# Output projection of a cross-attention block: seven block products per batch in place of eight

## The chip, the cores and the metric

The kernel runs on one core of a Trainium2 chip. The metric is the device time of one execution in microseconds (us), lower is better. Engines: PE is TensorE (matmuls), DVE is VectorE, ACT is ScalarE, POOL is GpSimd; the SP queue issues all DMA transfers here.

## The reference, cut to what matters

```
q = lora_linear(x, Wq, Aq, Bq)      # x: (8, 256, 1024), Wq: (1024, 1024)
k, v = lora_linear(traces, ...)     # 8 key/value heads of 32
attn = softmax(q k^T / sqrt(32)); context = attn v      # 32 query heads
out = lora_linear(context, Wo, Ao, Bo)                  # (8, 256, 1024)
return x + out
```

`lora_linear(x, W, A, B)` is `x @ W + 2 (x @ A @ B)` with rank 16. Everything is float32. The kernel folds the low-rank part into the weights first (W + 2AB), so that the last step is one product of the context, 256 x 1024 per batch, with a 1024 x 1024 matrix, called Wo below.

## The kernel before, in words

Every operand of a matmul is split into a high part (rounded to the format of the matmul) and a low part (the rest), and a product is the sum of three: high by high, high by low, low by high. So each 128-row step of a contraction is three matmuls.

The kernel has three stages. A prologue folds the weights and projects the first inputs. Then comes an attention stage of eight batches, cut into slots (32 per batch); in the last batch's slots the fold of Wo runs too, and the output projection of batch 0. At the end stands the output projection of batches 1 to 7 by itself.

Names that the change touches:

- `w_hl` (high, low) holds in its columns 512 to 1023 the right half of Wo, and `wkv_hl` the left half (`wo_piece`, line 282). The columns 0 to 511 of `w_hl` are free by then and take the context of two batches, `ctx_raw`, loaded by `load_ctx` (line 349). POOL makes Wo's low parts (line 644).
- `first_split` (line 696): POOL splits batch 1's context into `x_hl` (called `o_parts[1]`) in slots 28 and 31 to 33 of the last batch; its last step counts `o_ready`, on which PE's batch 1 waits.
- `place_max` (line 709), `normalize` (line 971, multiplies the context of one key/value head, "unit", by the row sums and counts `ctx_done`), `copy_turned` (line 964), `first_rows` (line 1013, adds x to the rows of batch 0). DVE's `slot` (line 1022) runs them in fixed slots: `first_rows` in slots 29, 33 and 37, `copy_turned` in 30 and 34, `normalize` of units 5, 6 and 7 in slots 31, 35 and 39.
- PE's `context` (line 1181) of unit 7 stands in slot 36, behind all of batch 0's output products, and waits until `normalize` of unit 6 has freed its bank.
- `out_batch` of PE (line 1296): four groups of 24 matmuls (`out_step`, line 1196), each 128 rows by 512 columns with the contraction over 1024: the two halves of the rows by the two halves of the columns. Each group has its own bank of PSUM, and two batches use different banks.
- `o_high` (ACT, line 864) and `o_low` (DVE, line 1069): one instruction each of 128 x 2048 elements splits the next batch's context into `c_hl` or `x_hl`. `rows_out` (DVE, line 1075): four additions of a bank and x's rows per batch. SP's `out_batch` (line 610) loads the next context but one, stores the rows and loads the next rows.

The order on each engine is written out by hand: an engine takes its instructions in program order, and a wait holds up all that stands behind it on that engine.

## Time and profile before

| | us |
|---|---|
| median of 3 runs (lowest, highest) | 716.83 (715.74, 717.96) |
| the profiled execution | 718.58 |
| its span, first to last instruction | 716.8 |
| PE busy | 697.4 |
| ACT busy | 446.3 |
| DVE busy | 400.9 |
| POOL busy | 310.3 |

The span is that of the profiled execution alone; 1.8 us lie around it. PE's busy time is modelled from starts of pipelined matmuls, so 97% says that it always has work queued, not that it runs at its peak.

### The profile page before, as it was taken

Reading aid. Unit: us, or ns where it says so; the run is one execution under the profiler, and the core shown is the slowest. Engines: PE = TensorE matmul, PEld = TensorE weight load, DVE = VectorE, ACT = ScalarE, POOL = GpSimd, SP = SyncE. Lnnn points to the kernel's source line nnn. Section 1 sums busy time; section 2 is a strip of 40 time slices with the busy share of each in tenths; the row PEclk is TensorE's granted clock in tenths of the full one; section 3 lists DMA queues with packets and bytes.
Section 4 is the critical chain, followed back from the end, with each engine's and each line's share of the span. In section 5 each row is a group of like instructions: output and inputs, shape, how many; then the busy total and the mean of one; then the engine's idle time right before and its main releaser. Section 6 shows DMA issues by size and latency. Waiting matters only on the chain.

```text
span 716.8 us, 16086 instructions
## 1 busy us (share of the span) xinstructions
PE 697.4 (97%) x5122; PEld 596.6 (83%) x5122; DVE 400.9 (56%) x805; ACT 446.3 (62%) x1418; POOL 310.3 (43%) x282
## 2 busy tenths in 40 slices
PE   6989999999999999999999999999899999999998
PEld 6768888888888888888888888887667788888886
DVE  4946877676566667567566656766674222122211
ACT  2546888888788788788888888888885111001100
POOL 3663832853573375277248338536878100000000
PEclk9999999999999999999999999999999999999999
DMA  6777675776577477666756757767675553354231
GB/s 231 274 222 210 196 199 148 192 192 180 153 187 202 136 198 199 168 159 186 197 140 187 196 146 191 196 175 193 179 221 198 170 176 110 125 176 160 74 117 59
DMA packets 103747, 125.77 MB, mean 175 GB/s; under 512 B 9248, under 2 KB 85280, under 8 KB 103712
## 3 DMA queue, kind: packets, MB, share of 16 engines
q1 hardware_dynamic: 103712, 125.34, 61.0%
q8 instruction: 17, 0.28, 0.2%
q14 instruction: 18, 0.15, 0.1%
HBM read 87.29 MB, written 38.01 MB: 175 GB/s over the span
## 4 chain that ended last, share of the span: by engine, by line
PE 87%; DMA 7%; DVE 2%; SPq 2%; POOL 1%; issue 1%; ACT 0%; DVEq 0%
PE banks L1131 35%; PE banks L1200 24%; PE banks L1149 10%; PE banks L1189 8%; PE banks L1176 8%; DMA r_rows<-turned_sb 3%; PE banks L1167 2%; PE banks L1116 1%; DMA probs_t<-b4kv 1%; DMA stage<-b4q 1%; POOL k_stack L654 1%; SPq L346 1%; DMA probs_t<-wq 1%; PE banks L1118 1%; DMA scales<-r_rows 1%
## 5 line engine op out<-in xcount | busy, mean ns | idle before, releaser
L943 DVE TENSOR_REDUCE neg_max<-banks 128x2 f32<-128x512 f32 x256 | 176.4, 690 | 130.3 <-PE banks L1149 128.8
L793 ACT ACTIVATE banks<-banks,neg_max 128x256 f32<-128x256 f32 x512 | 231.1, 455 | 15.5 <-DVE neg_max L943 15.5
L714 POOL TENSOR_TENSOR q_stack<-turned_sb,head_mask 8x512 fp32r<-8x512 f32 x128 | 135.6, 1060 | 202.1 <-DVE turned_sb L969 196.7
L804 ACT ACTIVATE probs_t<-banks 128x512 f32<-128x512 f32 x256 | 154.6, 604 | 74.0 <-PE banks L1176 72.4
L1131 PE MATMUL banks<-x_hi,w_hi 128*128 128x256 f32 x512 | 144.5, 282 | 0.9 <-POOL w_lo L644 0.9
L1131 PE MATMUL banks<-x_lo,w_hi 128*128 128x256 f32 x512 | 144.5, 282 | 0.0
L1131 PE MATMUL banks<-x_hi,w_lo 128*128 128x256 f32 x512 | 144.3, 282 | 0.0
L1149 PE MATMUL banks<-k_stack,q_stack 96*128 96x256 f32 x512 | 109.9, 296 | 3.9 <-DMA q_stack<-q_parts 2.5
L793 ACT ACTIVATION_READ_ACCUMULATOR banks<-banks,neg_max 128x1 f32 x512 | 108.6, 212 | 0.0
L1176 PE MATMUL banks<-q_stack,k_stack 104*128 104x512 f32 x256 | 107.7, 421 | 0.0
L1149 PEld LDWEIGHTS banks<-k_stack,q_stack 96*128 96x128 f32 x512 | 79.2, 190 | 31.6 <-ACT banks L793 19.8
L1131 PEld LDWEIGHTS banks<-x_lo,w_hi 128*128 128x128 f32 x512 | 97.4, 190 | 7.3
L1131 PEld LDWEIGHTS banks<-x_hi,w_hi 128*128 128x128 f32 x512 | 97.3, 190 | 1.4 <-issue 1.0
L1131 PEld LDWEIGHTS banks<-x_hi,w_lo 128*128 128x128 f32 x512 | 96.9, 189 | 0.0
L1083 DVE TENSOR_TENSOR raw<-banks,stage 128x512 f32<-128x512 f32 x28 | 19.4, 692 | 112.5 <-PE banks L1200 112.5
L1189 PE MATMUL banks<-probs_t,v_sb 128*32 128x256 f32 x1024 | 68.5, 385 | 0.0
L1176 PEld LDWEIGHTS banks<-q_stack,k_stack 104*128 104x128 f32 x256 | 48.4, 189 | 1.3 <-issue 0.8
L1189 PEld LDWEIGHTS banks<-probs_t,v_sb 128*32 128x32 f32 x1024 | 26.7, 109 | 20.7 <-issue 1.8
L867 ACT ACTIVATE x_hi<-w_hi 128x2048 fp32r<-128x2048 f32 x3 | 5.8, 1917 | 60.8 <-PE banks L1200 60.8
L693 POOL TENSOR_TENSOR c_lo<-raw,c_hi 128x512 fp32r<-128x512 f32 x32 | 41.3, 1291 | 2.5
L936 DVE TENSOR_TENSOR q_stage<-banks,q_stage 128x256 fp32r<-128x256 f32 x64 | 27.1, 424 | 25.7 <-ACT q_stage L777 25.2
L1131 PE MATMUL banks<-wkv_hi,c_hi 128*128 128x256 f32 x128 | 36.3, 284 | 1.1 <-DVE k_stage L931 1.1
(104 smaller groups left out, 1284.5 us busy)
## 6 DMA issues: line engine op xcount, KB each, us to landing
q_stack<-q_parts SPq DMA_DIRECT2D x192, 128.0 KB, 3.7
q_parts<-q_stage SPq DMA_DIRECT2D x64, 256.0 KB, 2.6
raw<-ct SPq DMA_DIRECT2D x32, 256.0 KB, 4.3
raw<-xt SPq DMA_DIRECT2D x32, 256.0 KB, 4.2
scales<-r_rows SPq DMA_DIRECT2D x64, 128.0 KB
context<-ctx_stage SPq DMA_DIRECT2D x64, 128.0 KB, 2.3
stage<-xn SPq DMA_DIRECT2D x16, 512.0 KB, 4.2
w_hi<-context SPq DMA_DIRECT2D x14, 512.0 KB, 6.0
```

The lines of the kernel that those rows point to most:

```text
L693: nc.gpsimd.tensor_tensor(cols[1], raw[:, j, :], cols[0], ALU.subtract).then_inc(ready, 1)
L714: nc.gpsimd.tensor_tensor(q_stack[rows, u % RING, heads], turned_sb[rows, u % 2].unsqueeze(1).broadcast_to([M_ROWS, 2, S]), head_mask[rows ...
L793: last = nc.scalar.activation(score_bank[c % 2][:, S * h:S * (h + 1)], score_bank[c % 2][:, S * h:S * (h + 1)], ACT.Exp, bias=neg_max[:, u ...
L804: nc.scalar.activation(probs_t[:, u % 2, t, 2 * hp:2 * hp + 2, :].rearrange("p a b -> p (a b)"), st_bank[j % 2], ACT.Exp, scale=-1.0).then ...
L936: nc.vector.tensor_tensor(q_stage[:, i % 2, 1, :], src, q_stage[:, i % 2, 0, :], ALU.subtract).then_inc(proj_out, 1)
L943: nc.vector.tensor_reduce(out=neg_max[:, u % 2, 2 * c:2 * c + 2], in_=score_bank[c % 2].rearrange("p (h t) -> p h t", h=2), axis=AXIS, op= ...
L1083: nc.vector.tensor_tensor(out_rows[h][:, cols], out_bank(i, h, half), x_rows[h][:, cols], ALU.add).then_inc(o_out, 1)
L1131: mm = nc.tensor.matmul(proj_bank[bank][:, 0:S], lhs, rhs, start=(k == 0), stop=(k == GROUP_MM - 1))
L1149: last = nc.tensor.matmul(score_bank[c % 2][:, S * h:S * (h + 1)], q_stack[0:3 * HD, u % RING, 2 * hp + h, P * qh:P * (qh + 1)], k_stack[0 ...
L1176: nc.tensor.matmul(st_bank[j % 2], k_stack[0:KM, u % NG, P * t:P * (t + 1)], q_stack[0:KM, u % RING, 2 * hp:2 * hp + 2, :].rearrange("p a ...
L1189: last = nc.tensor.matmul(ctx_bank[HD * h:HD * (h + 1), :], v_sb[:, t, HD * (u % NG):HD * (u % NG + 1)], probs_t[:, u % 2, t, h, :], start ...
L1200: mm = nc.tensor.matmul(bank, o_parts[i][t_part][:, kt, P * qh:P * (qh + 1)], wo_piece(w_part, kt, half), start=(k == 0), stop=(k == GROUP ...
```

## The change

For batches 2 to 7 the product of the context A (as 2 x 2 blocks of 128 x 512) and Wo (as B, 2 x 2 blocks of 512 x 512) is made from seven block products: A11 B11, A12 B21, S4 B22, A22 T4, S1 T1, S2 T2, S3 T3, with S1 = A21 + A22, S2 = S1 - A11, S3 = A11 - A21, S4 = A12 - S2 and T1 = B12 - B11, T2 = B22 - T1, T3 = B22 - B12, T4 = T2 - B21. Each block product is 12 matmuls of 512 columns. Batch 1 stays as it was, but for the order of its groups: both row halves of the right columns first.

POOL forms the S, ACT and DVE split each of the seven left factors (`form_high`, `form_low`) one product after the other, and DVE, POOL and ACT put the seven results together (`take_product`, `add_rows`, `copy_first`). The T are built once: T1's twelve pieces by DVE in slots 30 to 38 of the last attention batch, T2 and T4 by DVE after it, T3 by POOL. Banks, order and buffers are shown in the diff, cut to its core.

```diff
+PRODUCTS = (("A11", "B11", 0), ("S4", "B22", 1), ("S2", "T2", 6), ("A12", "B21", 7), ("S3", "T3", 2),
+            ("S1", "T1", 3), ("A22", "T4", 4))
+P1, P3, P6, P2, P7, P5, P4 = range(7)
+ADDED = ("S1", "S2", "S4", "S3")
+T1_SLOTS = (30, 31, 32, 32, 33, 34, 34, 35, 36, 36, 37, 38)
...
+        form_room = [q_stack[:, i].rearrange("p a b -> p (a b)") for i in range(4)] + [
+            k_stack[:, 4 * i:4 * i + 4].rearrange("p a b -> p (a b)") for i in range(2)] + [
+            q_stage[:].rearrange("p a b c -> p (a b c)")]
+        added_room = dict(zip(ADDED, [t[:].rearrange("p a b -> p (a b)") for t in (v_new, v_sb, ctx_stage, scales)]))
...
+        wo_forms = {"B11": [t[:, 0:4, :] for t in wkv_hl], "B21": [t[:, 4:8, :] for t in wkv_hl],
+                    "B12": [t[:, 0:4, 512:1024] for t in w_hl], "B22": [t[:, 4:8, 512:1024] for t in w_hl],
+                    "T1": [t[:].rearrange("p (a b) n -> p a (b n)", b=2) for t in c_hl],
+                    "T2": [t[:, 0:4, 512:1024] for t in w_hl],
+                    "T3": [w_hl[1][:, 4 * i:4 * i + 4, 0:512] for i in range(2)],
+                    "T4": [t[:].rearrange("p (a b) n -> p a (b n)", b=2) for t in x_hl]}
+        t1_raw = t4_raw = w_sum
+        t3_raw, t2_raw = (probs_t[:, i].rearrange("p a b n -> p (a b n)").rearrange("p (a n) -> p a n", a=4)
+                          for i in range(2))
+        u2, u3 = (t2_raw[:, i, :] for i in range(2))
...
+                for i in range(2):
+                    wait(ctx_stored[i], DMA * (1 + 4 * NG // 2))
+                wait(first_lo, 3)
+                wait(o_ready, 1)
+                load_ctx(3, 1)
...
+            for h in range(2):
+                wait(o_out, 7 + h)
+                sp.dma_start(out[1, P * h:P * (h + 1), :], out_rows[h]).then_inc(out_stored[h], DMA)
+                load_rows(2, h)
...
-                    wait(o_ready, v)
+                    wait(form_lo, products_to(v, P4))
...
+            pool.wait_ge(w_lo_pool, sums_to(FOLDS - 1))
+            pool.wait_ge(ctx_mm, (NB - 1) * NG + 7)
+            nc.gpsimd.tensor_tensor(t3_raw, wo_forms["B22"][0].bitcast(F32), wo_forms["B12"][0].bitcast(F32),
+                                    ALU.subtract).then_inc(t3_step, 1)
+            pool.wait_ge(t3_step, 1)
+            nc.gpsimd.tensor_tensor(t3_raw, t3_raw, wo_forms["B12"][1].bitcast(F32), ALU.subtract).then_inc(t3_step, 1)
+            def add_forms(v):
+                def a(name):
+                    return quarter(ctx_raw[v % 2], name)
+                pool.wait_ge(ctx_in[v % 2], (v + 1) // 2 * 2 * DMA)
+                if v > 2:
+                    pool.wait_ge(form_lo, products_to(v - 1, P5))
+                for n, (name, one, two, op) in enumerate((
+                        ("S1", a("A21"), a("A22"), ALU.add), ("S2", added("S1"), a("A11"), ALU.subtract),
+                        ("S4", a("A12"), added("S2"), ALU.subtract), ("S3", a("A11"), a("A21"), ALU.subtract))):
+                    nc.gpsimd.tensor_tensor(added(name), one, two, op).then_inc(form_added, 1)
+                    pool.wait_ge(form_added, 4 * (v - 2) + n + 1)
+            def add_rows(v):
+                def add(i, l, what):
+                    x = row_quarter(x_rows, i, l)
+                    nc.gpsimd.tensor_tensor(x, x, what, ALU.add).then_inc(rows_added, 1)
+                pool.wait_ge(copied, v - 1)
+                pool.wait_ge(rows_in[0], (v + 1) * DMA)
+                add(1, 1, p1_copy[:])
+                pool.wait_ge(p3_added, v - 1)
+                pool.wait_ge(u_done, 2 * (v - 2) + 1)
+                add(1, 2, u2)
+                pool.wait_ge(u_done, 2 * (v - 2) + 2)
+                pool.wait_ge(rows_in[1], (v + 1) * DMA)
+                add(2, 2, u3)
+                add(2, 1, u3)
+                pool.wait_ge(rows_added, 4 * (v - 1))
+            pool.wait_ge(ctx_done, NB * NG)
+            for i in range(2):
+                pool.wait_ge(ctx_stored[i], DMA * (1 + NB * NG // 2))
+            add_forms(2)
+            pool.wait_ge(t3_step, 2)
+            nc.gpsimd.tensor_tensor(t3_raw, t3_raw, wo_forms["B22"][1].bitcast(F32), ALU.add).then_inc(t3_step, 1)
+            pool.wait_ge(t3_step, 3)
+            pool.wait_ge(t_hi, 3)
+            nc.gpsimd.tensor_tensor(wo_forms["T3"][1], t3_raw, wo_forms["T3"][0], ALU.subtract).then_inc(t3_lo, 1)
+            for v in range(2, NB):
+                if v + 1 < NB:
+                    add_forms(v + 1)
+                add_rows(v)
...
-            def o_high(v):
-                act.wait_ge(ctx_in[v % 2], (v + 1) // 2 * 2 * DMA)
-                act.wait_ge(o_mm, 4 * (v - 1))
-                nc.scalar.activation(o_parts[v % 2][0][:].rearrange("p (a b) n -> p a (b n)", b=2), ctx_raw[v % 2],
-                                     ACT.Copy).then_inc(o_hi_done, 1)
+            def t_high(name, raw_tile, steps, count):
+                act.wait_ge(steps, count)
+                nc.scalar.activation(wo_forms[name][0], raw_tile, ACT.Copy).then_inc(t_hi, 1)
+            def form_high(v, p):
+                if v > 2:
+                    act.wait_ge(product_mm, products_to(v - 1, p))
+                name = PRODUCTS[p][0]
+                if name[0] == "A":
+                    act.wait_ge(ctx_in[v % 2], (v + 1) // 2 * 2 * DMA)
+                else:
+                    act.wait_ge(form_added, 4 * (v - 2) + ADDED.index(name) + 1)
+                nc.scalar.activation(form(p, 0), form_source(v, p), ACT.Copy).then_inc(form_hi, 1)
+            def copy_first(v):
+                act.wait_ge(product_mm, products_to(v, P1))
+                need(act, rows_added, 4 * (v - 3) + 1)
+                need(act, u_done, 2 * (v - 3) + 1)
+                nc.scalar.activation(p1_copy[:], product_bank(P1), ACT.Copy).then_inc(copied, 1)
+            act.wait_ge(st_mm, NB * SLOTS)
+            form_high(2, P1)
+            act.wait_ge(o_mm, 4)
+            t_high("T1", t1_raw[:], t_step, 12)
+            form_high(2, P3)
+            form_high(2, P6)
+            form_high(2, P2)
+            act.wait_ge(o_mm, 6)
+            act.wait_ge(t3_step, 1)
+            t_high("T2", t2_raw, t_step, 14)
+            form_high(2, P7)
+            form_high(2, P5)
+            for i in range(2):
+                act.wait_ge(q_stored[i], NB * 4 * DMA)
+            form_high(2, P4)
+            t_high("T3", t3_raw, t3_step, 3)
+            act.wait_ge(o_mm, 8)
+            t_high("T4", t4_raw[:], t_step, 16)
             for v in range(2, NB):
-                o_high(v)
+                for p in range(7):
+                    if p == P1:
+                        copy_first(v)
+                    if v + 1 < NB:
+                        form_high(v + 1, p)
...
+            def t1_piece(n):
+                op, kt = divmod(n, 4)
+                place = t1_raw[:, kt, :]
+                if n == 0:
+                    dve.wait_ge(w_lo_pool, sums_to(FOLDS - 1))
+                if op == 0:
+                    nc.vector.tensor_tensor(place, wo_forms["B12"][0][:, kt, :].bitcast(F32),
+                                            wo_forms["B11"][0][:, kt, :].bitcast(F32), ALU.subtract).then_inc(t_step, 1)
+                else:
+                    dve.wait_ge(t_step, n - 3)
+                    name, how = (("B12", ALU.add), ("B11", ALU.subtract))[op - 1]
+                    nc.vector.tensor_tensor(place, place, wo_forms[name][1][:, kt, :].bitcast(F32), how).then_inc(t_step, 1)
+            def t_total(base, taken, place, steps):
+                dve.wait_ge(t_step, steps)
+                nc.vector.tensor_tensor(place, wo_forms[base][0].bitcast(F32), taken, ALU.subtract).then_inc(t_step, 1)
+                dve.wait_ge(t_step, steps + 1)
+                nc.vector.tensor_tensor(place, place, wo_forms[base][1].bitcast(F32), ALU.add).then_inc(t_step, 1)
+            def t_low(name, raw_tile, highs):
+                dve.wait_ge(t_hi, highs)
+                nc.vector.tensor_tensor(wo_forms[name][1], raw_tile, wo_forms[name][0], ALU.subtract).then_inc(t_lo_dve, 1)
+            def form_low(v, p):
+                dve.wait_ge(form_hi, products_to(v, p))
+                nc.vector.tensor_tensor(form(p, 1), form_source(v, p), form(p, 0), ALU.subtract).then_inc(form_lo, 1)
...
+                if last:
+                    for n in range(len(T1_SLOTS)):
+                        if T1_SLOTS[n] == s:
+                            t1_piece(n)
...
+            def put_out(v, p, i, l, added):
+                if (i, l) in ((1, 1), (2, 2)):
+                    dve.wait_ge(out_stored[i - 1], (v + 1) * DMA)
+                dve.wait_ge(rows_added, 4 * (v - 2) + added)
+                nc.vector.tensor_tensor(row_quarter(out_rows, i, l), product_bank(p),
+                                        row_quarter(x_rows, i, l), ALU.add).then_inc(o_out, 1)
+            def take_product(v, p):
+                dve.wait_ge(product_mm, products_to(v, p))
+                if p == P3:
+                    x = row_quarter(x_rows, 1, 2)
+                    dve.wait_ge(rows_in[0], (v + 1) * DMA)
+                    nc.vector.tensor_tensor(x, product_bank(P3), x, ALU.add).then_inc(p3_added, 1)
+                if p == P6:
+                    dve.wait_ge(copied, v - 1)
+                    need(dve, rows_added, 4 * (v - 3) + 2)
+                    nc.vector.tensor_tensor(u2, product_bank(P6), p1_copy[:], ALU.add).then_inc(u_done, 1)
+                if p == P2:
+                    put_out(v, P2, 1, 1, 1)
+                if p == P7:
+                    dve.wait_ge(u_done, 2 * (v - 2) + 1)
+                    need(dve, rows_added, 4 * (v - 2))
+                    nc.vector.tensor_tensor(u3, product_bank(P7), u2, ALU.add).then_inc(u_done, 1)
+                if p == P5:
+                    put_out(v, P5, 2, 2, 3)
+                    put_out(v, P5, 1, 2, 2)
+                if p == P4:
+                    put_out(v, P4, 2, 1, 4)
+            dve.wait_ge(ctx_mm, NB * NG)
+            t_total("B22", t1_raw[:], t2_raw, 12)
+            t_low("T1", t1_raw[:], 1)
+            dve.wait_ge(t_lo_dve, 1)
+            t_total("B21", t2_raw, t4_raw[:], 14)
+            form_low(2, P1)
+            plain_rows(0)
+            plain_rows(1)
+            dve.wait_ge(t3_step, 2)
+            t_low("T2", t2_raw, 2)
+            form_low(2, P3)
+            form_low(2, P6)
+            plain_rows(2)
+            form_low(2, P2)
+            form_low(2, P7)
+            form_low(2, P5)
+            plain_rows(3)
+            t_low("T4", t4_raw[:], 4)
+            form_low(2, P4)
+            for v in range(2, NB):
+                for p in range(7):
+                    take_product(v, p)
+                    if v + 1 < NB:
+                        form_low(v + 1, p)
...
-            out_batch(1, 1, True)
-            pe.wait_ge(o_out, 4)
-            with pe.Fori(1, NB // 2) as pair:
-                for i in range(2):
-                    out_batch(pair * 2 + i, i, False)
+            pe.wait_ge(o_ready, 1)
+            for n in range(4):
+                if n == 2:
+                    pe.wait_ge(ctx_done, NB * NG)
+                for k in range(GROUP_MM):
+                    out_step(1, out_bank(n), n % 2, 1 - n // 2, k)
+            def product(v, p):
+                weight = PRODUCTS[p][1]
+                pe.wait_ge(form_lo, products_to(v, p))
+                if v == 2 and p == P6:
+                    pe.wait_ge(t_lo_dve, 2)
+                if v == 2 and p == P7:
+                    pe.wait_ge(t3_lo, 1)
+                if v == 2 and p == P4:
+                    pe.wait_ge(t_lo_dve, 3)
+                if v == 2 and p in (P1, P7):
+                    pe.wait_ge(o_out, 4 if p == P1 else 8)
+                if v > 2:
+                    free = {P1: (copied, v - 2), P3: (p3_added, v - 2), P6: (u_done, 2 * (v - 3) + 1),
+                            P2: (o_out, 4 * (v - 1) + 1), P7: (u_done, 2 * (v - 2)),
+                            P5: (o_out, 4 * (v - 1) + 3), P4: (o_out, 4 * v)}[p]
+                    pe.wait_ge(*free)
+                for k in range(12):
+                    kt, part = divmod(k, 3)
+                    w_part, a_part = ((0, 0), (0, 1), (1, 0))[part]
+                    mm = nc.tensor.matmul(product_bank(p), form_room[p][:, 512 * a_part + P * kt:512 * a_part + P * (kt + 1)],
+                                          wo_forms[weight][w_part][:, kt, :],
+                                          start=(k == 0), stop=(k == 11))
+                mm.then_inc(product_mm, 1)
+            for v in range(2, NB):
+                for p in range(7):
+                    product(v, p)
```

## Rows read from the trace of the kernel before

**Rows 1.** The page's busy times, and its chain that ended last, by engine.

```profile
PE 697.4 (97%) x5122; PEld 596.6 (83%) x5122; DVE 400.9 (56%) x805; ACT 446.3 (62%) x1418; POOL 310.3 (43%) x282
...
PE 87%; DMA 7%; DVE 2%; SPq 2%; POOL 1%; issue 1%; ACT 0%; DVEq 0%
```

**Rows 2.** The chain from 560 us to the end: start, us, what.

```profile
559.95 1.00 PE banks L1189 x16
560.95 152.60 PE banks L1200 x672
713.55 0.02 issue
713.58 0.69 DVE raw L1083
```

**Rows 3.** The windows view: us, PE, PEld, DVE, ACT, POOL busy, granted clock, DMA share, GB/s.

```profile
10.00:15.00 5.00, 1.35 (x4) 1.20 (x5) 4.51 (x3) 1.26 (x2) 3.32 (x2) 0.83 0.70 267
15.00:17.00 2.00, 2.00 (x9) 1.74 (x8) 0.41 (x1) 0.84 (x2) 0.00 (x0) 0.58 0.00 0
...
590.00:600.00 10.00, 10.00 (x46) 8.29 (x45) 1.25 (x2) 0.00 (x0) 0.00 (x0) 1.00 0.39 130
```

**Rows 4.** Groups by line: engine, operation, out<-in, shape, count, busy, mean ns, idle before.

```profile
L644 POOL TENSOR_TENSOR w_lo<-w_sum,w_hi 128x512 fp32r<-128x512 f32 x16 | 20.6, 1285 | 10.2 <-ACT w_hi L770 9.7
L1083 DVE TENSOR_TENSOR raw<-banks,stage 128x512 f32<-128x512 f32 x28 | 19.4, 692 | 112.5 <-PE banks L1200 112.5
...
L770 ACT ACTIVATE w_hi<-w_sum 128x512 fp32r<-128x512 f32 x16 | 10.2, 636 | 3.5 <-DVE w_sum L913 3.5
...
L1073 DVE TENSOR_TENSOR c_lo<-w_hi,c_hi 128x2048 fp32r<-128x2048 f32 x3 | 6.9, 2292 | 3.2 <-ACT c_hi L867 3.2
...
L867 ACT ACTIVATE x_hi<-w_hi 128x2048 fp32r<-128x2048 f32 x3 | 5.8, 1917 | 60.8 <-PE banks L1200 60.8
```

**Rows 5.** POOL's timeline at four moments at which it meets DVE.

```profile
18.08 1.53 POOL L644 TENSOR_TENSOR wkv_lo<-w_sum,wkv_hi 128x512 fp32r<-128x512 f32 x1 [4.69 <-ACT wkv_hi L770]
...
24.79 5.84 POOL L654 TENSOR_TENSOR q_stack<-stage,q_stack 32x1024 fp32r<-32x1024 f32 x2 [0.63 <-DVE q_stack L881]
...
154.80 2.54 POOL L714 TENSOR_TENSOR q_stack<-turned_sb,head_mask 8x512 fp32r<-8x512 f32 x2 [2.28 <-DVE turned_sb L969]
...
532.76 4.03 POOL L644 TENSOR_TENSOR w_lo<-w_sum,w_hi 128x512 fp32r<-128x512 f32 x3
```

**Rows 6.** DVE's timeline at the same four moments.

```profile
17.79 0.68 DVE L981 TENSOR_TENSOR c_lo<-raw,c_hi 128x512 fp32r<-128x512 f32 x1
18.39 0.68 DVE L913 SCALAR_TENSOR_TENSOR w_sum<-banks,probs_t 128x512 f32<-128x512 f32 x1
...
25.08 3.30 DVE L885 TENSOR_TENSOR q_stack<-stage,q_stack 64x1024 fp32r<-64x1024 f32 x1
...
156.58 1.30 DVE L981 TENSOR_TENSOR x_lo<-raw,x_hi 128x512 fp32r<-128x512 f32 x1
...
535.58 0.69 DVE L913 SCALAR_TENSOR_TENSOR w_sum<-banks,raw 128x512 f32<-128x512 f32 x1
```

**Rows 7.** POOL's timeline, 546 to 559 us.

```profile
546.78 1.04 POOL L701 TENSOR_TENSOR x_hi<-w_hi,ones 128x512 fp32r<-128x512 f32 x1
547.91 1.29 POOL L704 TENSOR_TENSOR x_lo<-w_hi,x_hi 128x512 fp32r<-128x512 f32 x1
549.27 2.16 POOL L714 TENSOR_TENSOR q_stack<-turned_sb,head_mask 8x512 fp32r<-8x512 f32 x2
...
557.35 1.29 POOL L704 TENSOR_TENSOR x_lo<-w_hi,x_hi 128x512 fp32r<-128x512 f32 x1
```

**Rows 8.** DVE's timeline, 542 to 562 us: start, us, engine, line, what.

```profile
547.41 0.42 DVE L969 COPY turned_sb<-banks 104x256 f32<-104x256 f32 x1 [1.46 <-PE banks L1167]
...
550.79 0.42 DVE L975 TENSOR_TENSOR ctx_stage<-banks,scales 128x256 f32<-128x256 f32 x1 [2.85 <-DMA scales<-r_rows]
552.37 0.69 DVE L1019 TENSOR_TENSOR stage<-banks,stage 128x512 f32<-128x512 f32 x1 [1.15 <-PE banks L1200]
...
555.66 0.41 DVE L975 TENSOR_TENSOR ctx_stage<-banks,scales 128x256 f32<-128x256 f32 x1
560.06 0.69 DVE L1019 TENSOR_TENSOR stage<-banks,stage 128x512 f32<-128x512 f32 x1 [3.98 <-PE banks L1200]
561.08 0.42 DVE L975 TENSOR_TENSOR ctx_stage<-banks,scales 128x256 f32<-128x256 f32 x1 [0.33 <-PE banks L1189]
```

**Rows 9.** DMA issues: what, queue, count, KB each, median us to landing.

```profile
context<-ctx_stage SPq DMA_DIRECT2D x64, 128.0 KB, 2.3
```

**Rows 10.** PE's timeline, 10 to 30 us: its first work behind its longest idle time there.

```profile
13.65 1.19 PE L1116 MATMUL banks<-probs_t,half_ident 128*128 128x256 f32 x2 [4.26 <-POOL k_stack L654]
```

More of the change, by code:

```diff
@@ L211, in xattn @@
         ctx_done = sem("ctx_done")
-        o_hi_done = sem("o_hi_done")
+        form_added = sem("form_added")
+        form_hi = sem("form_hi")
+        form_lo = sem("form_lo")
+        t_step = sem("t_step")
+        t3_step = sem("t3_step")
+        t_hi = sem("t_hi")
+        t_lo_dve = sem("t_lo_dve")
+        t3_lo = sem("t3_lo")
+        product_mm = sem("product_mm")
+        copied = sem("copied")
+        rows_added = sem("rows_added")
+        p3_added = sem("p3_added")
+        u_done = sem("u_done")
         first_hi = sem("first_hi")
@@ L301, in lora_of, with out_bank, product_bank, products_to @@
             return lora_q if f < FOLD_O else lora_o
-        def out_bank(i, qh, half):
-            return banks[:, ((0, 6, 1, 7), (2, 3, 4, 5))[i][2 * qh + half], :]
+        def out_bank(n):
+            return banks[:, 2 + n, :]
+        def product_bank(p):
+            return banks[:, PRODUCTS[p][2], :]
+        def products_to(v, p):
+            return 7 * (v - 2) + p + 1
+        def quarter(raw_tile, name):
+            i, j = int(name[1]) - 1, int(name[2]) - 1
+            return raw_tile.rearrange("p a (h n) -> p a h n", h=2)[:, 2 * j:2 * j + 2, :, P * i:P * (i + 1)]
+        def form_source(v, p):
+            name = PRODUCTS[p][0]
+            if name[0] == "A":
+                return quarter(ctx_raw[v % 2], name)
+            return added(name)
+        def added(name):
+            return added_room[name].rearrange("p (a h n) -> p a h n", a=2, h=2)
+        def form(p, part):
+            return form_room[p][:, 512 * part:512 * (part + 1)].rearrange("p (a h n) -> p a h n", a=2, h=2)
+        def row_quarter(rows, i, l):
+            return rows[i - 1][:, 512 * (l - 1):512 * l]
         def need(engine, semaphore, value):
@@ L1067, in _ @@
                 dve.sem_inc(out_stored[h], DMA)
-            def o_low(v):
-                i = v % 2
-                dve.wait_ge(o_hi_done, v - 1)
-                hi, lo = (t[:].rearrange("p (a b) n -> p a (b n)", b=2) for t in o_parts[i])
-                nc.vector.tensor_tensor(lo, ctx_raw[i], hi, ALU.subtract).then_inc(o_ready, 1)
-            def rows_out(v, i):
-                for h in range(2):
-                    dve.wait_ge(rows_in[h], v * DMA + DMA)
-                    dve.wait_ge(out_stored[h], v * DMA + DMA)
-                    for half in range(2):
-                        dve.wait_ge(o_mm, v * 4 + (2 * h + half + 1))
-                        cols = slice(512 * half, 512 * (half + 1))
-                        nc.vector.tensor_tensor(out_rows[h][:, cols], out_bank(i, h, half),
-                                                x_rows[h][:, cols], ALU.add).then_inc(o_out, 1)
@@ L1086, in _, with plain_rows @@
-            dve.wait_ge(o_ready, 1)
-            for v in range(1, NB):
-                if v + 1 < NB:
-                    o_low(v + 1)
-                rows_out(v, v % 2)
+            def plain_rows(n):
+                half, h = 1 - n // 2, n % 2
+                if half == 1:
+                    dve.wait_ge(rows_in[h], 2 * DMA)
+                    dve.wait_ge(out_stored[h], 2 * DMA)
+                dve.wait_ge(o_mm, 4 + n + 1)
+                cols = slice(512 * half, 512 * (half + 1))
+                nc.vector.tensor_tensor(out_rows[h][:, cols], out_bank(n), x_rows[h][:, cols],
+                                        ALU.add).then_inc(o_out, 1)
@@ L1294, in _ @@
                 slot(NB - 1, s, False, True)
-            def out_batch(v, i, first):
-                pe.wait_ge(o_ready, v)
-                for qh in range(2):
-                    if first and qh:
-                        pe.wait_ge(ctx_done, NB * NG)
-                    for half in range(2):
-                        if not first:
-                            pe.wait_ge(o_out, v * 4 + (2 * qh + half - 7))
-                        for k in range(GROUP_MM):
-                            out_step(i, out_bank(i, qh, half), qh, half, k)
```

23 lines of the change are left out of this document (12 added, 11 removed).

## The prediction

> **What bounds the kernel now.** I read the page's busy times first, then the chain that ended last, then the chain in order of time for the end. PE is busy for 97% of the span and carries 87% of the chain [rows 1]. From 560.95 us on the chain is one piece, 672 matmuls of the output projection in 152.60 us, with 0.02 us of idle, one DVE addition and a store of some 2.5 us behind it [rows 2]. So here PE's matmuls alone set the time, at 152.60 / 672 = 0.227 us each, and the other engines have room: in ten of these microseconds DVE works 1.25 and POOL not at all [rows 3]. The chain passes through `context` of unit 7 at 559.95 [rows 2]. All that the change adds comes before or after that point, on DVE, POOL and ACT.
>
> **What it removes.** Batches 2 to 7 take 7 x 12 = 84 matmuls in place of 96, so 6 x 12 = 72 fall away: 72 x 0.227 = 16.3 us, all on PE's path. That is certain if PE is never kept waiting.
>
> **What it adds when all runs smoothly.** A block product is 12 x 0.227 = 2.72 us and a batch 19.0. Per batch ACT gets eight operations of 512 columns (0.64 each, 5.1 us), DVE seven low parts and seven additions (0.69 each at most [rows 4], 9.7 us), POOL eight additions (1.28 each, 10.3 us). A left factor is split a whole batch ahead, right behind the product that freed its room, so about 13 us of slack hide it. From batch 3 on I cost this at nothing; its cover is that slack. Context loads now hang on the last low part of a batch, some 19 us before they are needed, with a store and a row load beside them as before: nothing. The last addition and the half-row store at the end stay: nothing. The longer unrolled code I bound between 0 and 1 us and take 0, as batch 1, unrolled already, sits inside the same 152.60 us.
>
> **Where it costs: DVE and POOL in each other's way.** Rows 5 and 6 have to be read together. DVE's `L885` at 25.08 starts inside two POOL operations and takes 3.30 us; its work of 1024 columns is about 1.1. It ends 2.2 us late, when the first POOL operation is through. The POOL pair takes 5.84, and 1.1 of that is DVE's, for which the second stood still: 2.4 us for each. `L981` at 156.58 takes 1.30 in place of 0.68 and ends 0.54 behind POOL's pair, whose end is 157.34. The other way round, POOL's `L644` at 18.08 takes 1.53 in place of 1.28, for `L981` at 17.79 was still at work. But `L913` at 535.58 takes 0.69 in the middle of POOL's 4.03 us of work: it reads a bank and one tensor of SBUF [rows 5, 6]. So a DVE operation on two SBUF tensors and a POOL operation exclude each other, each for its whole length, and whoever waits gets the next turn; additions from PSUM are exempt. Page "SBUF — State Buffer" of the Trainium skill, section "SBUF: two separate sides", calls the pair of ports an exclusive lock, "held for the full instruction"; by that rule the trace agrees for lengths up to 2.4 us, and no row shows a longer one.
>
> All of T1 to T4, every low part of a factor, every S and every row sum on POOL now lies in this queue. Prices of a turn: DVE 0.60 for 512 columns (starts of successive operations at 17.79 and 18.39 [rows 6]) and 2.2 for 2048 (2.29 less the overlap [rows 4]); POOL 1.24 for 512 (1.28 [rows 4] less overlap). POOL on 2048 is not in the trace. Lower bound 4 x 1.04 = 4.2 from the scaling operation, upper bound 4 x 1.29 = 5.2 [rows 7]; I take 4.9, 1.28 plus three more times the 1.2 that lie between 512 and the 2.4 us of 1024 columns. Page "GPSIMD Engine Reference" of the Trainium skill, section "Elementwise — side-by-side cycle accounting", has 4.5 us for this operation; by it the end would come about 1.6 us earlier than by the rows.
>
> I write the queue out, with 0.1 us where an engine waits for its own last result, and with turns alternating where both want one.
>
> 1. **To `context` of unit 7.** DVE's first T1 piece is at 547.8, behind `copy_turned` [rows 8]. Behind `normalize` of unit 5 (at 550.8 [rows 8]) stand pieces 1 to 6 and then `normalize` of unit 6, and each piece waits for one POOL operation of `place_max` and `first_split`, eight operations that follow each other almost without a gap from 549.27 to 558.64 [rows 7]: piece 1 ends at 552.6, piece 3 at 556.1, piece 6 at 561.2, `normalize` at 561.6 in place of 556.1 [rows 8]. PE wants it at 559.95 [rows 2]: it waits 1.7, and batch 1 starts at 562.7. POOL's last low part of batch 1, `o_ready`, comes at 562.5, just in time.
> 2. **To `ctx_done`.** Piece 7 ends at 563.1. POOL's two first T3 steps, 4.9 each, alternate with pieces 8 and 9: 574.1. `first_rows` (0.6), pieces 10 and 11 (1.2) and `normalize` of unit 7 (0.4) end at 576.3. PE's third group of batch 1 waits for it: due at 562.7 + 48 x 0.227 = 573.6, so 2.8 lost. Queued behind are SP's last context store (0.3 + 2.3 us [rows 9]) and with it POOL's S of batch 2, from 579.
> 3. **To the first product.** Four passes of T2 and T4 and T1's low part are 5 x 2.2, four S of POOL stand between them (4 x 1.24), then P1's low part: 11.0 + 5.0 + 0.6 = 16.6, done at 593.0. PE is through with batch 1 at 587.2: 5.8 lost. It works on P1 until 595.7.
> 4. **To the second product.** T3's third step 592.9 to 597.8, T2's low part to 600.0, T3's low part (its high part, 1.92 on ACT [rows 4], is ready at 599.9) to 604.9, P3's low part to 605.5. PE starts P3 at 605.6, 9.9 us late by the rows at full clock.
> 5. **After it.** The six low parts left of batch 2 come at 0.6 each with 2.72 us of need each: no stall. T4's low part and POOL's S of batch 3 make DVE some 6 us late, less than the slack of a factor. Per later batch the queue holds 8 x 1.3 + 7 x 0.6 = 14.6 of 19.0 us, so it catches up.
> 6. **The clock.** PE idles 4.26 us before 13.65 [rows 10], and the granted clock is 0.83 in 10 to 15 us and 0.58 in 15 to 17: partly at 1.2 in place of 2.4 GHz, which loses 0.17 x 5 + 0.42 x 2 = 1.7 us of full-speed work [rows 3]. The waits of 5.8 and 9.9 us are longer than that idle time. Bounds: nothing, or 1.7 us for each. For the one ahead of P3 I take 1.7, as its row is so near; the one ahead of P1 costs nothing, because P3 waits for DVE anyway.
>
> Sum: -16.3 + 1.7 + 2.8 + 5.8 + 9.9 + 1.7 = +5.6; counted from P3's start (41 products in 111.5 us, the clock, 3.2 us of tail) the span ends at 722.1, or +5.3. The profiled execution took 718.58 with its span of 716.8; with the change it would take 724. It stands 1.75 above the median of the runs, 716.83, so the median becomes 722. Should P3's low part get its turn ahead of T3's, a matter of 0.2 us, PE starts P3 at 600.7, waits 2.8 for P6, and the end is near 718.5. I forecast **721.0**.
>
> **Rivals.**
> - *DVE keeps its turn* as long as its operations follow each other without a wait. No row shows both queues full. Then pieces 2 and 3, 5 to 7 and so on go together, `normalize` comes in time, but POOL's last low part of batch 1 comes at 567.7 only, PE starts batch 1 6.8 late and P3 at 600.1 us: 716.9, no change, give or take 2. Chance 0.27.
> - *The turns are not whole ones*: long POOL operations let DVE in between, or the three engines' work falls more luckily than I wrote. With no collision at all DVE has P1's low part at about 574 and P3's at about 580, ahead of PE's 582.7 and 585.4, and the full saving stands: 716.8 - 16.3, a median of 700.5. Against it stand all of [rows 5, 6]; for it, that none shows an operation of 4.9 us. Chance 0.18, over 700 to 713.
> - *The queue never recovers*: POOL lags into batch 4 and later, and stalls come back in each batch. It decides from the point where the queue holds over 19.0 us a batch, and I count 14.6. Then over 724: chance 0.05.
> - My forecast, alternating turns: 0.5, from 718.5 to 723.5.
>
> **How the numbers follow.** A measurement of this kernel tells 0.3%, 2.15 us, from no change. Slower by more (over 719.0): most of the forecast and the last rival, 0.5. Within it (714.7 to 719.0): most of the first rival and the lucky end of mine, 0.28. Faster: the rest, 0.22. The range runs from 713.0, below which only the second rival lies, to 724.0. It takes in POOL's bounds (4.2 gives about 2.8 us less, 5.2 about 1.2 more) and the clock's.
>
> **What the profile after would show.** If I am right: T1's pieces of over 1 us while POOL works, two of them near 5; `context` of unit 7 waiting for `normalize`; PE's P3 of batch 2 waiting for DVE some 5 to 10 us; `t_low` and `t_total` well over 2.3 us, POOL's long steps up to 7; from P6 of batch 2 on, gapless PE, 2.72 us a product; a granted clock below 1 behind the longest wait. Wrong: T1's pieces at 0.68 beside a busy POOL, or PE without a gap at batch 2, and then 700.5.

## The result, and the profile after

The changed kernel takes 720.31 us (median of 17 runs, 718.42 to 723.64), the kernel before, measured beside it, 717.96 (17 runs). The ratio is 1.0039, 95% interval 1.0026 to 1.0052: slower by 2.35 us, within the range and 0.7 us below the number forecast. The 72 matmuls are gone and their 16.3 us with them; 18.7 us came back.

The profiled execution took 719.19 us with a span of 717.4, 0.6 more than the span of before. Busy time and the chain by engine, from the page of the changed kernel:

```profile
PE 685.9 (96%) x5050; PEld 585.6 (82%) x5050; DVE 484.6 (68%) x878; ACT 470.7 (66%) x1464; POOL 414.5 (58%) x334
...
PE 78%; DMA 7%; DVE 7%; issue 2%; POOL 2%; SPq 2%; ACT 1%; DVEq 0%; POOLq 0%
```

Against [rows 1], PE is busy for 11.5 us less, but its share of the chain fell from 87% to 78%, and DVE's rose from 2% to 7%. DVE's busy time grew by 83.7 us for 73 more instructions, 1.15 us each, and POOL's by 104.2 for 52, 2.0 each. DVE's 73 are, on balance, 72 of 512 columns and one of 2048, which alone take some 0.7 us each on average; POOL's are 48 of 512 and four of 2048, some 1.5 us each on average (estimates from 0.68 and 2.29, and from 1.28 and the 4.62 of the last experiment). So both engines are busy for longer than their new work is: a first sign that some of it is waiting.

The chain in order of time shows where it left PE. P1, P3, P6, P2, P7, P5 and P4 below are the seven block products in the order in which PE makes them: A11 B11, S4 B22, S2 T2, A12 B21, S3 T3, S1 T1 and A22 T4. These are rows of the chain of the changed kernel from 565 us on (start, us, what):

```profile
565.06 5.08 DVE w_sum L1200
570.15 0.60 DVE stage L1185
...
572.31 1.71 DMA context<-ctx_stage
...
574.24 1.41 POOL v_new L848
...
587.58 4.98 DVE q_stack L1216
592.55 1.20 DVE raw L1277 x2
593.75 2.20 DVE w_lo L1212
595.95 4.95 DVE q_stack L1216
...
600.95 113.20 PE banks L1567 x492
...
714.17 0.69 DVE raw L1285
```

Where [rows 2] had one piece of 672 matmuls, there is now one of 492 (41 products) from 600.95 on. Ahead of it the chain runs through DVE, and two of its steps are low parts of 512 columns, work of 0.6 us, that last 5. PE's own timeline, 556 to 625 us, has just four rows with idle time ahead of them (in brackets, with what released PE):

```profile
558.82 1.07 PE L1433 MATMUL banks<-probs_t,v_sb 128*32 128x256 f32 x16 [0.17 <-DVE ctx_stage L1141]
...
572.34 0.50 PE L1444 MATMUL banks<-wkv_hi,x_hi 128*128 128x512 f32 x1 [1.34 <-DVE ctx_stage L1141]
...
592.61 1.22 PE L1567 MATMUL banks<-wkv_hi,q_stack 128*128 128x512 f32 x2 [9.08 <-DVE q_stack L1216]
...
600.95 1.22 PE L1567 MATMUL banks<-w_hi,q_stack 128*128 128x512 f32 x2 [3.27 <-DVE q_stack L1216]
```

They are the four waits of the prediction: `context` of unit 7, the third group of batch 1, P1 and P3. Together 13.9 us. None follows, to the end.

The reason is in two timelines, to be read side by side. DVE's, changed kernel, 556 to 602 us (start, us, engine, line, operation, out<-in, shape, count):

```profile
560.04 10.11 DVE L1200 TENSOR_TENSOR w_sum<-w_sum,wkv_lo 128x512 f32<-128x512 f32 x2
...
572.21 2.27 DVE L1206 TENSOR_TENSOR probs_t<-w_hi,w_sum 128x2048 f32<-128x2048 f32 x1
574.52 3.27 DVE L1208 TENSOR_TENSOR probs_t<-probs_t,w_lo 128x2048 f32<-128x2048 f32 x1
...
584.41 3.24 DVE L1208 TENSOR_TENSOR w_sum<-w_sum,wkv_lo 128x2048 f32<-128x2048 f32 x1
587.58 4.98 DVE L1216 TENSOR_TENSOR q_stack<-w_hi,q_stack 128x512 fp32r<-128x512 f32 x1
...
593.68 2.27 DVE L1212 TENSOR_TENSOR w_lo<-probs_t,w_hi 128x2048 fp32r<-128x2048 f32 x1
595.88 5.02 DVE L1216 TENSOR_TENSOR q_stack<-ctx_stage,q_stack 128x512 fp32r<-128x512 f32 x1
600.82 0.68 DVE L1216 TENSOR_TENSOR q_stack<-v_sb,q_stack 128x512 fp32r<-128x512 f32 x1
```

POOL's, the same stretch:

```profile
556.40 1.49 POOL L775 TENSOR_TENSOR x_hi<-w_hi,ones 128x512 fp32r<-128x512 f32 x1
557.96 1.61 POOL L778 TENSOR_TENSOR x_lo<-w_hi,x_hi 128x512 fp32r<-128x512 f32 x1
559.52 5.07 POOL L832 TENSOR_TENSOR probs_t<-w_hi 128x2048 f32<-128x2048 f32 x1
564.67 4.93 POOL L835 TENSOR_TENSOR probs_t<-probs_t,w_lo 128x2048 f32<-128x2048 f32 x1
574.24 1.40 POOL L848 TENSOR_TENSOR v_new<-w_hi 128x512 f32<-128x512 f32 x1 [4.64 <-DMA context<-ctx_stage]
575.71 3.22 POOL L848 TENSOR_TENSOR v_sb<-v_new,w_hi 128x512 f32<-128x512 f32 x1
...
582.31 3.19 POOL L848 TENSOR_TENSOR scales<-w_hi 128x512 f32<-128x512 f32 x1
585.58 6.42 POOL L875 TENSOR_TENSOR probs_t<-probs_t,w_lo 128x2048 f32<-128x2048 f32 x1
594.09 6.26 POOL L878 TENSOR_TENSOR w_lo<-probs_t,w_lo 128x2048 fp32r<-128x2048 f32 x1 [2.09 <-ACT w_lo L995]
```

Two pieces of T1 take 10.11 us beside POOL's first two steps of T3, and the two low parts of 5 us lie under its last two. A pass of 2048 columns takes 2.27 alone (572.21) and 3.24 to 3.37 when an S of POOL must go first; the S takes 3.2 in place of 1.3. The time shows as busy time of the operation that stands still, not as a wait: DVE's "busy" 4.98 us hold 0.6 of work.

### The profile page after: what moved, and what is told of

Its sections match the earlier page's. It is cut to its first block, busy times and chain, and to the rows that moved or that the text cites. A ratio compares the mean times of both kernels' runs of the same rounds, so it can differ in the third digit from the quotient of the medians.

```text
span 717.4 us, 16217 instructions
## 1 busy us (share of the span) xinstructions
PE 685.9 (96%) x5050; PEld 585.6 (82%) x5050; DVE 484.6 (68%) x878; ACT 470.7 (66%) x1464; POOL 414.5 (58%) x334
## 4 chain that ended last, share of the span: by engine, by line
PE 78%; DMA 7%; DVE 7%; issue 2%; POOL 2%; SPq 2%; ACT 1%; DVEq 0%; POOLq 0%
PE banks L1375 35%; PE banks L1567 16%; PE banks L1393 9%; PE banks L1433 8%; PE banks L1420 7%; DMA r_rows<-turned_sb 3%; PE banks L1411 2%; DVE w_sum L1200 1%; DVE q_stack L1216 1%; DMA q_parts<-q_stage 1%; DMA q_stack<-q_parts 1%; PE banks L1360 1%; DMA probs_t<-b4kv 1%; POOL k_stack L728 1%; PE banks L1362 1%
## 5 line engine op out<-in xcount | busy, mean ns | idle before, releaser
L856 POOL TENSOR_TENSOR stage<-stage,probs_t 128x512 f32<-128x512 f32 x18 | 27.2, 1527 | 29.6 <-DVE probs_t L1304 19.8
L1567 PE MATMUL banks<-wkv_hi,q_stack 128*128 128x512 f32 x96 | 31.3, 408 | 9.1 <-DVE q_stack L1216 9.1
L757 POOL TENSOR_TENSOR x_hi<-raw,ones 128x512 fp32r<-128x512 f32 x28 | 31.5, 1126 | 11.6 <-PE banks L1375 8.3
```

Of the source, the lines that this page charges most:

```text
L757: nc.gpsimd.tensor_tensor(hi, raw[:, j, :], ones[:, 0:1].broadcast_to([P, 2 * S]), ALU.mult).then_inc(hi_done, 1)
L856: nc.gpsimd.tensor_tensor(x, x, what, ALU.add).then_inc(rows_added, 1)
L1567: mm = nc.tensor.matmul(product_bank(p), form_room[p][:, 512 * a_part + P * kt:512 * a_part + P * (kt + 1)], wo_forms[weight][w_part][:, k ...
```

## The experiments

**T3 on 16 of every 512 columns.** It leaves out nearly all of T3, so what P7 multiplies with is not T3; all instructions and waits remain. If POOL's long operations are the cause, this alone brings back the saving. The rival: DVE's own list before P1 (five passes of 2048) is too long whatever POOL does.

```diff
-            nc.gpsimd.tensor_tensor(t3_raw, wo_forms["B22"][0].bitcast(F32), wo_forms["B12"][0].bitcast(F32),
+            few = slice(0, 16)
+            nc.gpsimd.tensor_tensor(t3_raw[:, :, few], wo_forms["B22"][0][:, :, few].bitcast(F32), wo_forms["B12"][0][:, :, few].bitcast(F32),
                                     ALU.subtract).then_inc(t3_step, 1)
...
```

> POOL's four T3 operations work on 16 of every 512 columns; most of T3 is left out, all waits and all else stay. Queue theory (an addition of two SBUF tensors on DVE and a POOL operation exclude each other): the four holds of 4.4 us go, norm of unit 7 comes 8 us sooner, PE has no gap at batch 2 (0 to 1 us in place of 9.1 and 3.3), the span falls from 717.4 to about 700. Rival, DVE's own list of work is too long (11 us of T2, T4 and T1 passes ahead of the first low part): T3 is not on DVE, so the gaps ahead of P1 and P3 stay above 8 us in sum and the span above 711.

Measured: 700.95 us (4 runs, 700.67 to 703.15), ratio to the kernel before 0.9785 [0.9753, 0.9816], span 698.9. DVE's timeline:

```profile
559.54 1.54 DVE L1201 TENSOR_TENSOR w_sum<-w_sum,wkv_lo 128x512 f32<-128x512 f32 x2
...
575.35 3.27 DVE L1209 TENSOR_TENSOR w_sum<-w_sum,wkv_lo 128x2048 f32<-128x2048 f32 x1
578.55 0.81 DVE L1217 TENSOR_TENSOR q_stack<-w_hi,q_stack 128x512 fp32r<-128x512 f32 x1
```

The pieces take 1.54 in place of 10.11 and P1's low part 0.81 in place of 4.98. The passes beside an S keep their 3.27 and do no harm: PE runs from 559.40 through batch 1 and 42 products without a gap. The rival fell. Four operations of POOL, some 18 us of its time, cost the whole saving and more: 2.35 slower than the kernel before with them, 17.1 faster without them.

**Fills in place of T3.** Is it that POOL is busy, or that it reads SBUF? Each step of T3 becomes two fills with zero of its 2048 columns, 3.7 us in all, that write as before but read nothing. T3 is left out.

```diff
-            nc.gpsimd.tensor_tensor(t3_raw, wo_forms["B22"][0].bitcast(F32), wo_forms["B12"][0].bitcast(F32),
-                                    ALU.subtract).then_inc(t3_step, 1)
-            pool.wait_ge(t3_step, 1)
-            nc.gpsimd.tensor_tensor(t3_raw, t3_raw, wo_forms["B12"][1].bitcast(F32), ALU.subtract).then_inc(t3_step, 1)
+            marks = [0, 0]
+            for _ in range(2):
+                nc.gpsimd.memset(t3_raw, 0.0).then_inc(t3_step, 1)
+                marks[0] += 1
+                pool.wait_ge(t3_step, marks[0])
...
```

> Each of POOL's four T3 operations is replaced by two fills of the same 2048 columns with zero, about 3.7 us in all: POOL is busy for nearly as long, but reads nothing. T3 is left out (zeros). If the two engines exclude each other over reading: DVE's T1 pieces beside the fills take 0.68 us, PE has no gap at batch 2 and the span is near 700, as with the thinned T3. If any POOL operation shuts DVE out: two T1 pieces take about 2 us each (a fill apiece), and 5 to 8 us of gaps stay, span 707 to 713.

Measured: 700.79 us (4 runs, 700.52 to 704.77), ratio 0.9791 [0.9751, 0.983], span 698.7. POOL's timeline:

```profile
558.88 3.68 POOL L834 MEMSET probs_t<- 128x2048 f32 x2
562.62 3.70 POOL L838 MEMSET probs_t<- 128x2048 f32 x2
```

DVE's, beside it:

```profile
559.40 1.28 DVE L1209 TENSOR_TENSOR w_sum<-w_sum,wkv_lo 128x512 f32<-128x512 f32 x2
...
562.74 2.27 DVE L1215 TENSOR_TENSOR probs_t<-w_hi,w_sum 128x2048 f32<-128x2048 f32 x1
```

Under 7.4 us of fills, DVE's additions of two SBUF tensors take 0.64 and 2.27, their time alone. So POOL does not shut DVE out by being busy or by writing; what the fills lack is the reading of SBUF. The fills run in pairs of 1.85 us; had each shut DVE out, the two pieces would have taken about 2 us each.

**T3 in four operations a step.** The same work in turns a quarter as long. If turns go by whole instructions, P1 and P3 come much earlier.

```diff
-            nc.gpsimd.tensor_tensor(t3_raw, wo_forms["B22"][0].bitcast(F32), wo_forms["B12"][0].bitcast(F32),
-                                    ALU.subtract).then_inc(t3_step, 1)
-            pool.wait_ge(t3_step, 1)
-            nc.gpsimd.tensor_tensor(t3_raw, t3_raw, wo_forms["B12"][1].bitcast(F32), ALU.subtract).then_inc(t3_step, 1)
+            for kt in range(4):
+                nc.gpsimd.tensor_tensor(t3_raw[:, kt, :], wo_forms["B22"][0][:, kt, :].bitcast(F32),
+                                        wo_forms["B12"][0][:, kt, :].bitcast(F32), ALU.subtract).then_inc(t3_step, 1)
+            pool.wait_ge(t3_step, 4)
...
```

> Each T3 operation of 2048 columns in four of 512, same result, all else the same. Queue theory: POOL's work stays, but DVE gets a turn after each 1.1 us, so the T1 pieces take 1.6 in place of 5, the third group of batch 1 no longer waits, P1's low part comes some 6 us sooner and P3's gap grows to about 7: gaps of 10 us in sum in place of 13.9, no clock loss or 1.7, span 711 to 714. Rival, POOL's total work decides and not the length of a turn: no change, 717.

Measured: 714.8 us (10 runs, 712.97 to 716.16), ratio 0.9963 [0.9946, 0.998], span 711.6. PE's timeline, rows with idle time:

```profile
584.43 1.22 PE L1573 MATMUL banks<-wkv_hi,q_stack 128*128 128x512 f32 x2 [3.27 <-DVE q_stack L1222]
...
593.36 1.06 PE L1573 MATMUL banks<-w_hi,q_stack 128*128 128x512 f32 x2 [3.44 <-DVE q_stack L1222]
...
604.72 2.97 PE L1573 MATMUL banks<-w_lo,k_stack 128*128 128x512 f32 x12 [1.30 <-issue]
```

P1 waits 3.27 in place of 9.08. P3 waits 3.44, about as long as before and not the 7 expected, but starts 7.6 us earlier; ahead of its low part DVE now sat idle for 3.54 us until ACT had T2's high part. The row at 604.72 is P7, which needs T3; POOL's last piece of T3 ended at 604.62, though the trace names no releaser. Same work on the same engines, 5.5 us shorter by the medians: the length of a turn matters. The stall does not vanish, for the four turns together are about as long as the one was (4 x 1.0 against 4.5 us, an estimate), and DVE's passes now stand between them: the second step of T3 takes 11.5 us in place of 4.9, and POOL's first S starts at 577.2 in place of 574.2. The waits add up to 8.2 us in place of the 10 expected, but P1's twelve matmuls took 5.5 us in place of 2.7, at a granted clock of 0.65 from 586 to 592, so the span came out in the expected range all the same.

**DVE's order alone.** P1's, P3's and P6's low parts ahead of the passes, T4's two passes last.

```diff
+            form_low(2, P1)
             t_total("B22", t1_raw[:], t2_raw, 12)
             t_low("T1", t1_raw[:], 1)
-            dve.wait_ge(t_lo_dve, 1)
-            t_total("B21", t2_raw, t4_raw[:], 14)
-            form_low(2, P1)
             plain_rows(0)
+            form_low(2, P3)
+            form_low(2, P6)
             plain_rows(1)
...
```

> Only DVE's order at the start of the last stage is changed: the low parts of P1, P3 and P6 stand ahead of T4's two passes, P1's ahead of everything, the additions of batch 1 between. Same result. Queue theory: P1 and P3 no longer wait, the queue's work shows up later, as gaps of about 3.5 ahead of P6, 2 ahead of P2 and 3.5 ahead of P7, none long enough to cost clock: 10.8 us in sum, span near 711. If the order did not matter (the sum of work decides) it would stay at 717; if only the first gaps counted it would be near 703.

Measured: 714.61 us (10 runs, 711.42 to 719.21), ratio 0.9965 [0.9937, 0.9994], span 711.4. PE's timeline:

```profile
591.60 1.19 PE L1567 MATMUL banks<-w_hi,q_stack 128*128 128x512 f32 x2 [3.75 <-DVE w_lo L1212]
...
602.88 4.32 PE L1567 MATMUL banks<-w_lo,k_stack 128*128 128x512 f32 x12 [2.87 <-DVE raw L1277]
```

P1 and P3 no longer wait; P6 waits for T2's low part. P7, at 602.88, waits for the last addition of batch 1, which frees its bank and which this order puts behind T4's two passes; T3 itself was ready at 595.9. All waits together are 7.2 us, not the 10.8 expected. The span of 711.4 met the expected 711 by luck, since the expectation had no loss of clock: behind the wait of 3.75 us the 24 matmuls of P6 and P2 took 8.4 us in place of 5.4 (granted clock 0.66 from 592 to 600), and from P7 on 456 matmuls took 105.27 us, where the run before, at full clock, had 103.62. So order moves the stall to where some of it is covered. That no order takes it away is not shown: this one still held P7 back by DVE's list alone.

**PE kept busy through the two waits.** 36 and 20 matmuls into a free bank, in front of P1's and P3's waits; nothing else changes. It prices the clock.

```diff
+                if v == 2 and p in (P1, P3):
+                    for _ in range(36 if p == P1 else 20):
+                        nc.tensor.matmul(banks[:, 7, :], lora_o_sb[:, 0, 0:P], lora_o_sb[:, 0, 0:512], start=True, stop=True)
                 pe.wait_ge(form_lo, products_to(v, p))
```

> The changed kernel with 36 matmuls more ahead of the wait for P1's factor of batch 2 and 20 more ahead of the wait for P3's, on operands that no longer change, into a bank that nothing reads: they fill 8.2 and 4.5 us of the two gaps (9.1, and 5.6 if P1 runs at full clock). If the granted clock falls because PE sits idle, it stays 1.00 here, P3 still starts near 601 and the 41 products behind it take 111.5 in place of 113.2 us: 1.5 to 1.9 us faster than the changed kernel of the same call. If the clock falls for another reason, or the cost lay elsewhere: no change.

Beside it ran **the changed kernel once more**, for a second look at its clock on the same chip.

> The changed kernel as it is, on the same chip as the one kept busy, so that the two can be compared: a median near 720.3, gaps of 9.1 and 3.3 us ahead of P1 and P3 of batch 2, and a granted clock below 1 behind them.

Measured: 718.9 us with the filler (11 runs), ratio 1.001 [0.9992, 1.0029]; 719.73 without (12 runs), ratio 1.0029 [1.0011, 1.0046]. The windows view (us, PE, PEld, DVE, ACT, POOL busy, granted clock, DMA share, GB/s), first without the filler, in this second profile:

```profile
583.00:592.00 9.00, 0.04 (x1) 0.00 (x0) 8.97 (x3) 4.25 (x6) 8.46 (x2) 0.66 0.00 1
592.00:601.00 9.00, 5.41 (x13) 4.04 (x14) 9.00 (x7) 4.39 (x4) 6.26 (x1) 0.69 0.01 3
601.00:610.00 9.00, 9.00 (x30) 7.11 (x29) 9.00 (x9) 0.06 (x1) 6.18 (x4) 0.70 0.67 237
610.00:620.00 10.00, 10.00 (x46) 8.29 (x45) 8.71 (x13) 3.12 (x6) 7.80 (x5) 1.00 0.31 102
```

and with it:

```profile
583.00:592.00 9.00, 9.00 (x41) 7.47 (x40) 8.97 (x3) 5.04 (x7) 8.84 (x3) 1.00 0.01 3
592.00:601.00 9.00, 7.96 (x35) 6.23 (x34) 9.00 (x5) 4.78 (x4) 6.91 (x2) 1.00 0.00 1
601.00:610.00 9.00, 8.18 (x37) 6.41 (x36) 9.00 (x9) 0.00 (x0) 5.22 (x3) 1.00 0.54 188
```

The last piece of PE in the chain, first without and then with the filler:

```profile
600.49 114.58 PE banks L1567 x492
```

```profile
602.99 111.87 PE banks L1570 x492
```

With PE busy the granted clock stays at 1.00, though it still waits 1.04 us for P1's factor and 0.82 for P3's; with 9.1 us of idle time the mean is 0.66 to 0.70 from 583 to 610, some of it at 1.2 in place of 2.4 GHz, and full speed is back only some microseconds after P3 has begun. The 41 products from P3 on take 111.87 us with the filler, 113.20 and 114.58 without: 1.3 and 2.7 us. The medians lie only 0.8 apart, where 1.5 to 1.9 was expected, and their intervals overlap, so the end-to-end price of the clock is not settled more closely than "one or two microseconds".

**Strassen from batch 3 on.** Batch 2 goes by eight products and four free banks; T3 stands wholly behind the S, the low parts ahead of T1's, T2's and T4's, and T1 and T4 exchange their rooms. PE gives up one batch's saving, 12 x 0.227 = 2.7 us, and the T have one more batch of cover.

```diff
+V0 = 3
...
-            for v in range(2, NB):
+            for v in range(V0, NB):
...
+            o_low()
             t_total("B22", t1_raw[:], t2_raw, 12)
+            form_low(3, P1)
+            plain_rows(1, 0)
+            form_low(3, P3)
+            form_low(3, P6)
...
```

> A version meant to beat both: seven products for batches 3 to 7 only, batch 2 plain as before, so that the building has 43 us of PE's work above it in place of 22. T1 goes to x_hl and T4 to c_hl, all of T3 behind the S, and DVE's order follows the due times. Same result. Queue theory: 60 matmuls saved, 13.6 us; the queue holds some 43 us of work between 563 and 607, due at 604 to 609: gaps of 1 to 2 us in all, no clock loss, a span near 704 and a median near 706, 0.983 of before. If DVE and POOL are simply too slow for seven products, gaps come back ahead of P1 or P6 of batch 3 and the time stays above 712.

Measured: 705.66 us (5 runs, 704.48 to 705.85), ratio 0.9839 [0.9812, 0.9866], span 703.7; in all its output projection PE waits 1.0 us, in two waits. DVE's timeline:

```profile
576.36 5.10 DVE L1219 TENSOR_TENSOR q_stack<-v_sb,q_stack 128x512 fp32r<-128x512 f32 x1
...
586.41 5.09 DVE L1219 TENSOR_TENSOR k_stack<-scales,k_stack 128x512 fp32r<-128x512 f32 x1
...
593.83 6.00 DVE L1215 TENSOR_TENSOR x_lo<-w_sum,x_hi 128x2048 fp32r<-128x2048 f32 x1
```

POOL's:

```profile
575.97 4.94 POOL L875 TENSOR_TENSOR probs_t<-w_hi 128x2048 f32<-128x2048 f32 x1
...
593.05 4.62 POOL L883 TENSOR_TENSOR w_lo<-probs_t,w_lo 128x2048 fp32r<-128x2048 f32 x1 [2.10 <-ACT w_lo L1000]
```

DVE stands still just as long under T3, 5.1 us for work of 0.6, and nobody waits for those low parts yet; all that is left of it at PE is at most the 1.0 us. This version beats both kernels: 11.4 us under the kernel before by the medians of its own comparison (717.05), and 14 to 15 under the changed one. It changes the start of the products, the place of T3 and DVE's order together; how much each brings is not separated.

## Why the prediction was right, and where a step was off

The forecast, slower by 5.3 from its own profiled execution and 721.0 as its middle, came out at +2.35 and 720.31. The signs it named are all there, and the mechanism is the one forecast. That 720.31 lies only 0.7 from 721.0 is in part luck: the forecast counted from a median of 716.83 for the kernel before, so it said +4.2, and the 17 runs put that median at 717.96; +2.35 is a little over half of +4.2. The time alone would not settle it either, as the first rival, no change give or take 2, reaches almost as far; the rows do.

**Who gets the next turn.** The steps rested on alternation: whoever waits goes next, even where the other engine's operations follow each other at once. It held. In POOL's rows an operation begins every 1.56 us (556.40, 557.96, 559.52), which is one of POOL's and one of DVE's pieces, and no two of either engine go together. The rival by which DVE keeps its turn asked for pieces 2 and 3 together, and fell; so did the one by which long operations of POOL let DVE in between: the 4.98 and 5.02 us of two short low parts speak against it, and the experiment on thin T3 shows the time that it asked for. The queue recovers, as step 5 said: from 600.95 on PE has no gap, so the last rival fell too.

**Steps 1 and 2, mis-sized.** 1.7 and 2.8 were forecast, 0.17 and 1.34 came. The terms were the turns. POOL's 512 columns hold the ports for about 1.0 us, not 1.24: 1.56 less DVE's 0.55. Its 2048 columns hold them for about 4.5, not 4.9: at 575.97 in the last experiment POOL gets its turn when DVE's previous operation ends, at about 576.4, and DVE's low part, ending at 581.4 with its own 0.6, got its turn at about 580.9. The row of 4.62, with no DVE operation on two SBUF tensors ahead of it, says the same. My extrapolation added 1.2 for each 512 columns, where the increments are 1.1. The Trainium skill, page "GPSIMD Engine Reference", section "Elementwise — side-by-side cycle accounting", has 4.5 us for this operation; the runs agree, and its number would have served better than the rows from shorter operations.

**Steps 3 and 4, right in sum, wrong in place.** I had 5.8 ahead of P1 and 9.9 ahead of P3; it was 9.08 and 3.27. The term that was off is the store of the last context half, counted from the start of DVE's first pass: 0.3 + 2.3 us in the prediction, 574.24 - 572.21 = 2.03 in the run, of which 1.71 is the store. In the prediction POOL's first S asks for its turn at 579.0, 0.5 after DVE's second pass began; in the run it asks at 574.24, 0.2 before the first pass ended, and goes ahead of the second. So POOL was one turn further on, its fourth S was through before DVE's fifth pass and not behind it, and the third step of T3 got its turn at 587.6, ahead of P1's low part in place of behind it. The two need the same turns in another order: from the end of batch 1 to P3's start 17.4 us passed (583.5 to 600.95), where the prediction has 18.4. This is read from the rows; no run changed the store alone. The sum did not hang on the order, as P3 starts when the whole list is done, whichever comes first; the two waits alone add up to 12.35 us and not 15.7, because P1's slow matmuls (below) fill 2.4 of them.

**P3's wait is itself understated by the clock.** P1's twelve matmuls took from 592.61 to 597.68, 5.1 us in place of 2.72, or 0.42 each in place of 0.227, nearly all at 1.2 GHz. As P3 waits for DVE to 600.9 in any case, that costs nothing, as step 6 said.

**The clock**, 1.7 forecast: 113.20 - 111.5 = 1.7 in the first profile, 3.1 in the second. Right for the first; the range of 0 to 1.7 was too narrow. Nor does it take a wait of 9 us: the run with DVE's order changed, expected to lose no clock, lost 3.0 us behind a wait of 3.75 and 1.6 behind one of 2.87.

**The sum.** From `context` of unit 7 on, by the profiled executions: waits of steps 1 and 2, 1.5; batch 1 around its restarts 0.6 slower (22.4 in place of 21.8); P1 and its two waits 17.4 - 2.7 = 14.7; the clock 1.7; together 18.5, less 16.3 gives +2.2. The rows have 713.55 - 559.95 = 153.60 before, and 714.15 - 558.65 = 155.50 after, +1.9. The attention stage happened to end 1.3 us earlier in the profiled execution of the changed kernel (558.65 against 559.95), which is why the spans differ by 0.6 only. That end moves from execution to execution: in the other profiles `context` of unit 7 starts between 558.1 and 560.65. The medians' +2.35 agrees with +1.9 to 2.2. Of the 3 us by which the worked sum, +5.3, was too high, nearly all is in steps 1 and 2.

## What to carry to other kernels

When work is put beside a bound engine, ask of each added operation which ports it takes and how long one instruction holds them, not how busy its engine is: here 18 us of reads on POOL stopped DVE's short operations, for which PE waited. Cut such operations short (5.5 us here), put them where nobody waits for the engine they block, or give up a little of the saving for more cover; with T3 moved back and the short operations ahead, one more batch of eight products bought 14 us here, the three together. An operation that lasts far longer than others of its shape is waiting, though the profile calls it busy.
